# Three weighted passes over a graph's edges: products of four rows on VectorE, gathers written out with source numbers read in place

## What is computed

```python
w = jnp.exp(e - emax[dst])
wsum = jax.ops.segment_sum(w, dst, n)
att = w / wsum[dst]
out = jax.ops.segment_sum(att[:, :, None] * h[src], dst, n)
```

## Time and profile before

| | us |
|---|---|
| median of 3 runs | 4060.08 |
| lowest and highest run | 4056.94, 4063.56 |
| span of the profiled execution, its own time | 5649.1 |
| TensorE busy, in the profiled execution | 3213.5 |
| VectorE busy | 2171.3 |
| ScalarE busy | 1527.5 |
| GpSimd busy | 2057.0 |

### The profile page before, as it was taken

How to read it: one execution, slowest core, us unless ns; L and a number is a source line. 1 busy time by engine, 2 the same in 40 slices (tenths; PEclk the granted TensorE clock), 3 DMA queues, 4 the chain that set the end, 5 groups by cost and what they waited for, 6 DMA issues and landing times. The chain is left out here.

```text
span 5649.1 us, 65353 instructions
## 1 busy us (share of the span) xinstructions
PE 3213.5 (57%) x16684; PEld 1917.1 (34%) x16685; DVE 2171.3 (38%) x5425; ACT 1527.5 (27%) x3235; POOL 2057.0 (36%) x2082
## 2 busy tenths in 40 slices
PE   2111233349849965446802654771744464999998
PEld 1111111115537743223701522341522233444444
DVE  5222100001239884447301744780654458121213
ACT  0133200000349953234200032460033345121212
POOL 4665677750030045562174055306045641000000
PEclk5555555559979976667755866895866676999999
DMA  9323410014345632222412511004622231313231
GB/s 377 110 92 96 112 34 25 25 51 130 113 118 149 147 95 82 83 86 94 180 32 60 148 21 21 12 6 138 186 59 81 84 107 57 107 60 107 61 106 42
DMA packets 327831, 522.03 MB, mean 92 GB/s; under 512 B 141885, under 2 KB 203030, under 8 KB 323956
## 3 DMA queue, kind: packets, MB, share of 16 engines
q1 hardware_dynamic: 214361, 306.27, 18.4%
q0 software_dynamic: 78896, 124.49, 8.4%
q10 hardware_dynamic: 34381, 89.16, 4.2%
HBM read 407.66 MB, written 115.58 MB: 93 GB/s over the span
## 5 line engine op out<-in xcount | busy, mean ns | idle before, releaser
L1042 PE MATMUL ps<-shared_sb,onehot 128*128 128x264 f32 (+1 forms) x1600 | 600.2, 493 | 385.0 <-issue 217.5
L2100 DVE TENSOR_TENSOR accum<-accum,ps 128x264 f32 (+1 forms) x1248 | 529.4, 424 | 536.7 <-issue 311.9
L1327 ACT ACTIVATE onehot<-iota,drel 128x128 f32<-128x128 f32 x1248 | 381.3, 388 | 1068.6 <-PE ps L965 701.2
L1102 PE MATMUL ps<-score_sb,shared_sb 128*128 128x512 f16 (+1 forms) x3150 | 629.2, 360 | 20.6 <-DVE shared_sb L2129 20.2
L682 POOL DMA_INDIRECT score_sb<-table,idx_a x192 | 200.7, 1045 | 944.9 <-issue 465.3
L1042 PEld LDWEIGHTS ps<-shared_sb,onehot 128*128 128x128 f32 x1600 | 316.5, 230 | 670.9 <-issue 606.7
L812 PE MATMUL ps<-resid_sb,shared_sb 128*128 128x512 f32 (+1 forms) x416 | 297.1, 803 | 371.0 <-issue 318.5
L642 POOL DMA_INDIRECT t_w<-early_sb x391 | 389.4, 996 | 284.4 <-DVE counts L1836 182.3
L682 POOL DMA_INDIRECT shared_sb<-table,idx_a x384 | 364.1, 948 | 250.7 <-ACT idx_a L1310 140.0
L659 POOL DMA_INDIRECT t_adj<-counts,early_sb x391 | 403.6, 1032 | 121.5 <-issue 121.5
L1102 PEld LDWEIGHTS ps<-score_sb,shared_sb 128*128 128x128 bf16 x3150 | 298.6, 99 | 343.5 <-DVE shared_sb L2129 14.7
(11 more groups left out here) (413 smaller groups left out, 5592.3 us busy)
## 6 DMA issues: line engine op xcount, KB each, us to landing
score_sb<-t_adj SPq DMA_DIRECT2D x105, 640.0 KB, 3.9
accum<-t_hot SPq DMA_DIRECT2D x208, 256.0 KB
t_w<-accum ACTq DMA_DIRECT2D x13, 3200.0 KB
t_hot<-shared_sb SPq DMA_DIRECT2D x104, 256.0 KB
resid_sb<-t_w SPq DMA_DIRECT2D x25, 1024.0 KB
shared_sb<-t_key SPq DMA_DIRECT2D x98, 256.0 KB
t_adj<-accum ACTq DMA_DIRECT2D x35, 640.0 KB
shared_sb<-t_adj SPq DMA_DIRECT2D x35, 640.0 KB, 9.1
```

Source lines behind the costliest of these rows:

```text
L1042: pe.matmul(ps[:, RING[(HU * h + u) % len(RING)], 0:w], onehot[:, h % 2 * HU + u, :], around[g][place(g, i, h)][:, u, 0:w], start=True, st ...
L1102: mm = pe.matmul(ps[:, 2 * (i % 3) + f, 0:w], h_gin[:, t, m, f * P:(f + 1) * P], ring["gin"][:, at % HOLD, c, 0:w], start=(t == 0 and m == ...
L1327: last = act.activation(onehot[:, h % 2 * HU + u, :], iota[:, 0:P], ACT.Abs, bias=drel[:, bass.ds(step + u, 1)], scale=-1.0)
L2100: dve.tensor_tensor(to, to, bank.unsqueeze(1), ALU.add).then_inc(step_acc, 1)
```

## The change

The order of the three passes on GpSimd and VectorE is rewritten; TensorE's part is the same.

- GpSimd: `gathers`, for `g` = 0 and 2, is written out over all 52 turns. Its index operand is `src_x` in place, `idx_a` is gone. Its wait for `idx_ready` becomes a wait on `step_mm` for the turn that used the buffer last (`freed_by`).
- ScalarE: the copies of source numbers (`index`, `first_indices`) are gone.
- VectorE: a turn's products are two instructions of four rows, 1024 columns, each counting `msg_ready` up by four. The first stands before add 1 of a turn, the second before add 5. All 52 turns are written out. The eight tile numbers are copied from their registers together at the head of a turn. The wait on `step_mm` is made at even steps only, for two steps at once; the wait on `step_acc` stays at every add. In `g` = 1 the fold of the next layer's score vectors comes after 27 turns instead of 24.

```diff
@@ -378,6 +376,15 @@
 
             return 5 + n % 3 if n < UNDER else 4 + n % 4
 
+        def buffer_of(g, n):
+
+            return n % (RG[g] // HU) + ((3, 0, 6)[g] if n // (RG[g] // HU) == LAPS[g] else 0)
+
+        def freed_by(g, n):
+
+            lap = RG[g] // HU
+            return n - lap if n // lap < LAPS[g] else (LAPS[g] - 1) * lap + buffer_of(g, n)
+
         def product_out(kind, t):
 
             return count("l1_ev" if kind == "l1" else "node_sum", t + 1)
@@ -668,26 +675,7 @@
                     pool.sem_inc(done("pool_go"), 1)
                     pool.tensor_scalar(ends_at[0:EQ, i % 2, :], iota[0:EQ, :], carry_d[:, n:n + 1], None, ALU.is_equal).then_inc(done("ends_" + name), 1)
 
-            def gathers(g, tab, w, ready, n):
-
-                def four(i, c, first=False):
-
-                    if c >= 2:
-                        pool.wait_ge(*landed(g, i, c - 2))
-                    elif not first:
-                        pool.wait_ge(*landed(g, i - 1, RS // GU + c - 2))
-                    pool.sem_inc(done("pool_go"), 1)
-                    at = place(g, i, c // 2)
-                    for u in range(c % 2 * GU, c % 2 * GU + GU):
-                        pool.indirect_dma_start(around[g][at][:, u, 0:w], None, tab, bass.IndirectOffsetOnAxis(ap=idx_a[:, at * HU + u:at * HU + u + 1], axis=0)
-                                                ).then_inc(gath[c % NACC], 16)
-
-                def into(i, h, first=False):
-
-                    pool.wait_ge(idx_ready, (S // HU) * g + (RS // HU) * i + h + 1)
-                    pool.sem_inc(done("pool_go"), 1)
-                    four(i, 2 * h, first)
-                    four(i, 2 * h + 1, first)
+            def gathers(g, tab, w, ready, n_ready):
 
                 def looked_up():
 
@@ -695,17 +683,20 @@
                         pool.wait_ge(hot_kept[h], 16 * (S // QU // 2) + 16)
                     pool.wait_ge(*count("sc_dv", 2 + S // QU))
 
-                pool.wait_ge(*count(ready, n))
+                pool.wait_ge(*count(ready, n_ready))
                 pool.wait_ge(*count("kept", 16 * min(g + 1, 2)))
-                for h in range(RS // HU):
-                    if g == 0 and h == 8:
+                for n in range(S // HU):
+                    if g == 0 and n == 8:
                         looked_up()
-                    into(0, h, first=(g == 0 and h == 0))
-                with pool.Fori(1, LAPS[g]) as i:
-                    for h in range(RS // HU):
-                        into(i, h)
-                for h in range(LEFT[g]):
-                    into(LAPS[g], h)
+                    if n >= RG[g] // HU:
+                        pool.wait_ge(step_mm, RS + S * g + HU * freed_by(g, n) + HU)
+                    for c in (2 * n, 2 * n + 1):
+                        if g > 0 or c >= 2:
+                            pool.wait_ge(*landed(g, 0, c - 2))
+                        pool.sem_inc(done("pool_go"), 1)
+                        for u in range(c % 2 * GU, c % 2 * GU + GU):
+                            pool.indirect_dma_start(around[g][buffer_of(g, n)][:, u, 0:w], None, tab,
+                                                    bass.IndirectOffsetOnAxis(ap=src_x[:, n * HU + u:n * HU + u + 1], axis=0)).then_inc(gath[c % NACC], 16)
 
             def gathers_x():
 
...
@@ -1304,21 +1295,6 @@
                         act.activation(enc[:, q * QU:q * QU + QU, :], ps[:, 2:4, :].rearrange("p b (j d) -> p (b j) d", j=2),
                                        ACT.Relu).then_inc(done("enc_done"), 1)
 
-            def index(g, i, h):
-
-                at = place(g, i, h)
-                act.activation(idx_a[:, at * HU:at * HU + HU], src_x[:, bass.ds(i * RS + h * HU, HU)], ACT.Copy).then_inc(idx_ready, 1)
-
-            def first_indices(g):
-
-                if g == 1:
...
                 lap = RG[g] // HU
 
-                def after(i, h, to_index=None):
+                def after(i, h):
 
                     at = (i + (h + 2) // lap, (h + 2) % lap) if i is not LAPS[g] else (LAPS[g], h + 2)
                     act.wait_ge(msg_ready, S * g + RG[g] * i + HU * h + HU)
                     edge_weights(g, *at)
                     act.wait_ge(step_mm, RS + S * g + RG[g] * i + HU * h + HU)
-                    if to_index is not None and g != 1:
-                        index(g, *to_index)
                     one_hot(g, *at)
 
                 with act.Fori(0, LAPS[g] - 1) as i:
                     for h in range(lap):
-                        after(i, h, (i + 1, h))
+                        after(i, h)
                 for h in range(lap):
...
@@ -2073,49 +2044,50 @@
                 dve.tensor_tensor(alpha[:, far, 4:8], alpha[:, far, 0:4], peak[:, far, 0:4], ALU.mult).then_inc(done(f"weighted{k}"), 1)
 
             def add_up(g, w, H):
-                def weigh(i, h, u):
-
-                    turn = (S // HU) * g + (RG[g] // HU) * i + h
-                    now_w = ps[:, 5 + h % 2, 0:HU * 8].rearrange("p (u c) -> p u c", u=HU)
-                    if u == 0:
-                        dve.wait_ge(w_ready, turn + 1)
-                    if u % GU == 0:
-                        dve.wait_ge(*landed(g, i, 2 * h + u // GU))
-                    v = around[g][place(g, i, h)][:, u, 0:D].rearrange("p (h d) -> p h d", h=H)
-                    of_src = v if g != 1 else x_rows[h][:, u, :].unsqueeze(1).to_broadcast([P, H, DX])
-                    dve.tensor_tensor(v, of_src, now_w[:, u, 0:H].unsqueeze(2).to_broadcast([P, H, D // H]), ALU.mult).then_inc(msg_ready, 1)
-
-                def add(i, h, ahead=None):
-
-                    step = RG[g] * i + HU * h
-                    dve.load(tn_regs, tn_i[0:1, bass.ds(step, HU)])
+
+                lap = RG[g] // HU
+                turns = S // HU
+
+                def buffer_of(n):
+
+                    return place(g, LAPS[g], n % lap) if n // lap == LAPS[g] else n % lap
+
+                def weigh(n, half):
+
+                    now = slice(half * GU, half * GU + GU)
+                    if half == 0:
+                        dve.wait_ge(w_ready, turns * g + n + 1)
+                    dve.wait_ge(*landed(g, 0, 2 * n + half))
+                    now_w = ps[:, 5 + n % lap % 2, 0:HU * 8].rearrange("p (u c) -> p u c", u=HU)
+                    v = around[g][buffer_of(n)][:, now, 0:D].rearrange("p u (h d) -> p u h d", h=H)
+                    of_src = v if g != 1 else x_rows[n % lap][:, now, :].unsqueeze(2).to_broadcast([P, GU, H, DX])
+                    dve.tensor_tensor(v, of_src, now_w[:, now, 0:H].unsqueeze(3).to_broadcast([P, GU, H, D // H]), ALU.mult).then_inc(msg_ready, GU)
+
+                def add(n):
+
+                    dve.load(tn_regs, tn_i[0:1, HU * n:HU * n + HU])
+                    tiles = [dve.snap(r, min_val=0, max_val=NT - 1) for r in tn_regs]
                     for u in range(HU):
-                        if ahead is not None:
-                            weigh(*ahead, u)
-                        at = dve.snap(tn_regs[u], min_val=0, max_val=NT - 1)
-                        dve.wait_ge(step_mm, S * g + step + u + RS + 1)
-                        dve.wait_ge(step_acc, S * g + step + u + len(RING))
-                        bank = ps[:, RING[(HU * h + u) % len(RING)], 0:w]
-                        to = accum[:, bass.ds(at, 1), 0:w]
+                        if u % GU == 1 and n + 1 < turns:
+                            weigh(n + 1, u // GU)
+                        dve.wait_ge(step_acc, S * g + HU * n + u + len(RING))
+                        to = accum[:, bass.ds(tiles[u], 1), 0:w]
+                        if u % 2 == 0:
+                            dve.wait_ge(step_mm, S * g + HU * n + u + RS + 2)
+                        bank = ps[:, RING[(HU * (n % lap) + u) % len(RING)], 0:w]
                         dve.tensor_tensor(to, to, bank.unsqueeze(1), ALU.add).then_inc(step_acc, 1)
 
-                lap = RG[g] // HU
-                for u in range(HU):
-                    weigh(0, 0, u)
+                weigh(0, 0)
+                weigh(0, 1)
                 if g > 0:
                     far_weights(g)
                 else:
                     link(dve.memset(flat_a[:, 0:2048], 0.0))
                     dve.wait_ge(*count("exp0", 2))
-                with dve.Fori(0, LAPS[g] - 1) as i:
-                    for h in range(lap):
-                        add(i, h, (i + (h + 1) // lap, (h + 1) % lap))
-                if g == 1:
-                    fold(2, 4, P, (2, 3), "L2_gnn_a_src2", "L2_gnn_a_dst2", "ld_gat2")
-                for h in range(lap):
-                    add(LAPS[g] - 1, h, (LAPS[g], 0) if h == lap - 1 else (LAPS[g] - 1, h + 1))
-                for h in range(LEFT[g]):
-                    add(LAPS[g], h, (LAPS[g], h + 1) if h < LEFT[g] - 1 else None)
+                for n in range(turns):
+                    add(n)
+                    if g == 1 and n == 26:
```

(21 more changed lines are left out.)

## The result

| | us | against the kernel before |
|---|---|---|
| predicted | 4150, 4085 to 4225 | slower |
| kernel before, median of 20 | 4057.11 | |
| changed kernel, median of 20 | 4064.49 | 1.002 [1.0014, 1.0025] |
| its profiled execution | 4068.36, span 4066.5 | |

A forecast was written before the change was run, and what follows sets the result against it. The prediction took gathers to bind the outer passes (352 us) and VectorE the middle one (303); with VectorE needing 365 in each, +62 and twice +13 gave +88 on the timed median: 4150 us, range 4085 to 4225.

The forecast's parts named there:

- the gather time p = 1.05 us: GpSimd in timed runs: one gather takes 1.05 us, not the profiled 1.25, making outer passes 352 us.
- the 192 gathers ahead in the middle pass: Middle pass: 192 of 416 gathers ahead, the other 224 need at most 280 us, under VectorE's 298.
- the turn: VectorE's eight steps in a pass: 6.92 us against 5.73, 62 us more in 52 turns.
- the adds don't pay: Rival on VectorE: waiting adds start as soon as others, turn 5.6 us, total 4054 us; chance 0.06.
- reading in place: Gathers of the outer passes: dropping ScalarE's copies gains zero; without cover, 13 us a pass.
- the ring: Gather buffers of the outer passes: GpSimd is behind them where gathers bind, so neither the copy's wait nor its replacement matters.
- accounting of the 1589 us: Whole kernel: profiled excess split as 650 start, 488 outer passes, 195 middle, 310 look-ups; sum 1643, 54 over.
- Gathers still bound the outer passes: Rival, p of 1.25 us or anything from 1.09 on: only the middle pass grows, 4122 us; chance 0.26.
- Nothing happens, VectorE having slack in the middle pass too: Rival on the middle pass: VectorE has slack there too, so the time does not change; chance 0.04.
- The long records are real in timed runs: Rival on VectorE's sequencer: 0.70 us wait records also occur unprofiled, fewer records gain time, 4000 us; chance 0.08.
- The clock: Rival on TensorE: at half clock its turns of 7 to 9.8 us bind, 4250 us and more; chance 0.04.

The follow-up runs named there:

- before_third: The kernel before without an edit, traced in a short execution: 4059.71 us, ratio 1.0.
- before_again: The kernel before without an edit, traced in a long execution: 5606.42 us.
- gathers_only: The kernel before with only the written-out gathers reading source numbers in place, VectorE's part as before: 5603.46 us, ratio 0.9995, in long executions.
- half_before_second: The kernel before with two of each four gathers left out in all three passes, in short executions: 3816.97 us, ratio 0.9386.
- rows_in_middle: The changed kernel with VectorE's order of the kernel before in the middle pass alone: 5578.43 us, ratio 0.9956, in long executions.

## Why the prediction was wrong

The sum had +62 us for the middle pass and +13 for each outer one. Measured from first product to last add they came out as +11, -1 and -1 (362.7 for 351.9, 420.6 for 421.4, 419.2 for 420.3), and +7 on the time. Two steps failed: the gather time p = 1.05 us, which made the 26 us of the outer passes, and the 192 gathers ahead in the middle pass, which made VectorE its bound and is the larger error.

**Right: the turn.** Predicted 6.92 us, measured 6.87. Its terms: product 1.13 against 1.13, adds in a row 0.60 against 0.57, inside the bounds of 0.43 and 0.64, the add behind the load 0.98 against 1.06, inside 0.88 and 1.13, an add ahead of a product 0.34 against 0.34 and 0.35. The misses cancel in part, 5 x -0.03 + 0.08. That an add waiting for the one before costs more than a product beside it saves is shown twice: by the turn itself and by the 141 us of the pair without half of the gathers. The rival "the adds don't pay" is out, as rows 13 had said. The Trainium skill says in "VectorE: DVE Perf Modes", section "The DRAIN you can't avoid", of eight copies with a semaphore after each, that it "costs nothing extra here". That cannot be carried over to these adds, each of which also waits for the one before: 0.57 us apart, not 0.34.

**Right: reading in place is worth zero**, and in short executions its cover was the one named: gathers bind, and GpSimd is behind the ring (in `before_third` it waits for a copy of source numbers 4 times). In long ones it is not behind the ring: in `before_again` GpSimd waits for such a copy 43 times, 417 us in all, in `gathers_only` as long for TensorE's step, 413 us in 37 waits, and the 26 us of two passes without cover did not come either (5603.46 against 5605.04 us). What covers the copy there is not shown.

**Wrong, first: "What p is in a timed run", p = 1.05 us.** The prediction had 1.25 in its rows and 416 us for an outer pass by it; the passes are 422 and 421. It gave both up for an accounting of the 1589 us between the profiled execution and the timed ones. The traces of the kernel before of both kinds, `before_again` (long) and `before_third` (short), give the true one (first product to last add for a pass; the stretches add up to the spans of 5604.5 and 4058.6 us):

| stretch | long | short | difference | in the accounting |
|---|---|---|---|---|
| start to first product | 2082 | 1335 | 747 | 650 |
| first pass | 562 | 421 | 141 | 244 |
| to the middle pass | 586 | 329 | 257 | 310, with "to the third pass" |
| middle pass | 492 | 352 | 140 | 195 |
| to the third pass | 385 | 267 | 118 | in the 310 |
| third pass | 563 | 420 | 143 | 244 |
| rest | 934 | 935 | -1 | 0 |

The outer passes were given 204 us too much, which is what took them from 421 to 336, and the middle one 55; the start and the look-ups were given 97 and 65 too little. The errors cancelled to within a hundred, the sum met its target to 54 us by chance, and the 54 were then spread over gathers and scatters as though they were a measurement. The start was wrong in its mechanism too. It was to be shorter because scatters run at p = 1; they end at 1102 for 1228 and take 958 ns in both kinds. Of the 747 us, 430 lie ahead of the first gather (1538 and 1108) and 317 between it and the first product. What ends 690 us sooner are the first layer's matmuls of line 812, first the short execution, then the long one:

```profile
L812 PE MATMUL ps<-resid_sb,shared_sb x416: 590/592/1220, 409.0 to 634.4; 128*128 128x512 f32 x134, 98*128 98x512 f32 x5
```
```profile
L812 PE MATMUL ps<-resid_sb,shared_sb x416: 589/594/1222, 683.2 to 1324.0; 128*128 128x512 f32 x134, 98*128 98x512 f32 x5
```

The same 416 matmuls with the same median, spread over 225 or 641 us. And the trace that the prediction read was not one of passes bound by gathers: their last gathers start 54, 145 and 36 us ahead of the last adds, where in `before_third` it is 11.8, 11.6 and 11.7.

**Wrong, second: "The middle pass has 192 of its 416 gathers ahead, and the other 224 need at most 280 us".** 192 are ahead where the look-up comes behind the burst of gathers, in a long execution. In a short one it runs beside them, which the prediction itself assumed for the time of the look-ups, and did not carry over to the number of gathers ahead. 144 are ahead (143 in the changed kernel), and the other 272 need 272 x 1.25 = 340 us and 12 for the last landing and turn: 352 us, the measured length of the pass. (All 416, from 1898 on, take 1.27 us each with the gaps and end at 2426.) VectorE alone takes 302 us from its first add to its last (`half_before_second`, 1998.3 to 2299.9, where it never waits for rows in this pass). From its first add at 2089.5 it would have been done at 2391: it had 46 us to spare. With fours it takes 359 us, from 2084.9 to 2443.95, which is 57 more, begun 5 earlier. 57.4 - 4.7 - 45.9 = 6.8 us is what is left over, the middle pass ending at 2443.95 and not at 2437.11. (The sum closes whatever VectorE's own time is; what that time shows is that 46 of the 57 us fell into slack.) This is the whole cost: the third pass then starts 9 and ends 8 us later, the spans differ by 7.9 us and the medians by 7.4.

**The rivals.** *Gathers still bound the outer passes* named the right mechanism for two of three passes, with a chance of 0.26, and its 4122 us kept the error of the third. With the middle pass of the short trace, first product at 2085 and last add at 2437, the prediction's own 365 us for VectorE would have given 4060 + 2085 + 365 - 2437 = 4073 us. *Nothing happens, VectorE having slack in the middle pass too* came nearest in time and was held at 0.04 by "the full VectorE of rows 6", which is a row of a long execution's quiet end, when no gather was left (the pass's last one starts at 3603). *The long records are real in timed runs* is wrong for the compared times, where in `before_third` the record of line 2097 takes 21 ns among gathers too:

```profile
L2097 DVEq EVENT_SEMAPHORE  x135: 21/21/21, 2200.2 to 2299.6; - x135
```

and right for the long executions, which are timed runs as well: there fours shorten the last pass by 12 us, and `rows_in_middle` is 0.4 and 1% faster than the kernel before. The clock did not fall: TensorE's granted clock is 0.98 of 2.4 GHz in the changed middle pass, 0.92 before.

**Fours in the outer passes, rows product by row in the middle** was run three times. It is the faster kernel in long executions and equal to the kernel before in short ones (0.9995 [0.9986, 1.0004]). No version here with all its gathers beats the kernel before in short ones.

## What to carry to other kernels

Before pricing a change, ask for each stretch which of two producers is late at its end, and read it in the same kind of execution as the times. Here the distance from a pass's last gather to its last add tells it: 12 us where gathers bind, 20 us and more where they don't. When the profiled execution is far longer than the timed ones, do not fit a unit cost to the difference: a unit cost that stands in hundreds of rows, even and untouched by the disturbance, is better than one from a sum with terms missing. And four small products joined into one save 0.05 us each (0.33 against 1.13 / 4), while each add that loses the operation between it and the last pays 0.57 - 0.34 = 0.23; where accumulations wait for one another, the interleaving is worth more than the width.

## What was not expected of the hardware

- The same program has two kinds of executions, near 4060 and near 5605 to 5650 us, that last a whole occasion (30 of 30 executions of the kernel before long in the first two series, 41 of 42 short in the two later ones). The operations take the same time in both (scatters, gathers, the matmuls of line 812, VectorE's busy time of a pass); what differs in the traces is the sequencers' records, and idle time charged to the issue. In a long execution the wait record of line 2097 takes up to 0.71 us, here in `before_again` between 3300 and 3400, where the short one has 21 ns throughout:

```profile
L2097 DVEq EVENT_SEMAPHORE  x69: 2/21/710, 3300.6 to 3397.3; - x69
```

  What puts a chip into the one or the other was not tried and stays open.
- The 0.30 us between two gathers, with the issue as the releaser, is there for looped and for written-out gathers, for copied and for in-place source numbers, and in both kinds of executions. The Trainium skill says in "GPSIMD Engine Reference", section "Key points", that GpSimd is the only option for gathers; no run here tries another. At 1.25 us each the 1248 gathers take 1560 us of GpSimd's time, and they set where all three passes of the kernel before end in a short execution.
- With fewer and longer products TensorE's granted clock rose, from 0.84 to 0.90 in the first pass and from 0.92 to 0.98 in the middle one, and its busy time fell from 310 to 282 us and from 292 to 259. The outer passes are no shorter for it: their rows came no sooner.
